# A recurrence in units of two steps: paired values on two row groups of the array, one VectorE product for two

## The reference

```
o_t[j] = sum_i r_t[i] * (s[i,j] + exp(u[i] + k_t[i]) * v_t[j])
s[i,j] = exp(w_t[i]) * s[i,j] + k_t[i] * v_t[j]
```

## Time and profile before

| | us |
|---|---|
| Median of 3 runs | 2596.15 (2594.57 to 2597.19) |
| Profiled execution | 2599.8, span 2598.0 |
| A woven stage (seven) | 208.2 |
| Recurrence alone (last) | 153 |
| Busy: PE, DVE, ACT, POOL | 2043.4, 1638.1, 845.2, 607.8 |

### The profile page before, as it was taken

The page is one execution under the profiler, slowest core; times in us unless marked ns, Lnnn a source line. Parts: engine busy times, 40 slices in busy tenths (PEclk is TensorE's granted clock), DMA queues, the critical chain, the costliest instruction groups (busy, mean ns, idle before and its releaser), DMA issues. The chain is left out here.

```text
span 2598.0 us, 29698 instructions
## 1 busy us (share of the span) xinstructions
PE 2043.4 (79%) x10381; PEld 1319.8 (51%) x10444; DVE 1638.1 (63%) x2846; ACT 845.2 (33%) x1530; POOL 607.8 (23%) x357
## 2 busy tenths in 40 slices
PE   0865985896796797697599588655279999999998
PEld 0543554454354454454455445422157777777775
DVE  3234696696597588679569669658355555455554
ACT  0342352353333333344235235320133222322222
POOL 0000243143044033233224314315111220112010
PEclk9686897897897888789789789775589999999999
DMA  4000000000000000000000000000210000000000
GB/s 120 1 1 8 1 1 17 1 1 9 9 1 9 9 1 1 17 1 1 17 1 1 17 1 1 1 8 0 65 53 22 17 17 17 0 17 16 16 1 17
DMA packets 32290, 33.24 MB, mean 13 GB/s; under 512 B 4496, under 2 KB 31184, under 8 KB 31952
## 3 DMA queue, kind: packets, MB, share of 16 engines
q1 hardware_dynamic: 32144, 31.38, 3.9%
HBM read 22.99 MB, written 8.39 MB: 12 GB/s over the span
## 5 line engine op out<-in xcount | busy, mean ns | idle before, releaser
L557 DVE TENSOR_TENSOR_SCAN s_buf<-r_work,kvb 128x512 f32<-128x512 f32 x256 | 363.9, 1422 | 0.0
L655 POOL TENSOR_TENSOR p_buf<-s_buf,r_work 128x512 f32<-128x512 f32 x128 | 151.9, 1187 | 511.5 <-DVE s_buf L557 511.5
L1525 PE MATMUL mbank<-m_xh,w_hi 128*128 128x512 f32 x544 | 229.5, 422 | 0.1
L1333 DVE TENSOR_TENSOR hl<-hf,hh 128x512 fp32r<-128x512 f32 x136 | 94.0, 691 | 201.1 <-ACT hh L1440 200.4
L655 POOL TENSOR_TENSOR r_work<-s_buf,r_work 128x512 f32<-128x512 f32 x128 | 165.1, 1290 | 229.1 <-DVE s_buf L557 229.1
L710 ACT ACTIVATE probs<-bank_s,nmx 128x256 f32<-128x256 f32 (+1 forms) x512 | 186.9, 451 | 94.2 <-DVE nmx L420 90.6
L1525 PE MATMUL mbank<-m_xl,w_hi 128*128 128x512 f32 x544 | 216.5, 398 | 0.0
L1525 PE MATMUL mbank<-m_xh,w_lo 128*128 128x512 f32 x544 | 216.2, 397 | 0.0
L728 ACT ACTIVATE pt<-bank_s 128x1024 f32<-128x1024 f32 (+1 forms) x128 | 117.5, 918 | 248.5 <-PE bank_s L972 248.5
L546 DVE TENSOR_TENSOR kvb<-r_work,bank 128x512 f32<-128x512 f32 x256 | 174.7, 682 | 23.7 <-PE bank L1070 13.1
L1436 ACT ACTIVATE sg<-mbank 128x512 f32<-128x512 f32 x136 | 81.5, 599 | 327.6 <-PE mbank L1525 327.6
(11 more groups left out here) (247 smaller groups left out, 4155.0 us busy)
## 6 DMA issues: line engine op xcount, KB each, us to landing
w_raw<-in_w SPq DMA_DIRECT2D x17, 256.0 KB, 2.7
x_new<-in_x SPq DMA_DIRECT2D x8, 512.0 KB, 3.3
x_after_rwkv<-x_b SPq DMA_DIRECT2D x8, 512.0 KB, 3.7
m_x_tok<-x_after_rwkv SPq DMA_DIRECT2D x8, 512.0 KB, 3.8
out<-m_x_tok SPq DMA_DIRECT2D x8, 512.0 KB, 2.9
w_raw<-in_w2e SPq DMA_DIRECT2D x17, 128.0 KB, 2.7
work<-in_w SPq DMA_DIRECT2D x2, 1024.0 KB
wrk<-in_wrk SPq DMA_DIRECT2D x1, 1024.0 KB
```

The costliest lines, as they stand in the source:

```text
L557: V.tensor_tensor_scan(s_buf[:, n % 2, 1:S + 1], dec[:, n // HD, :], kvb[:, n % 2, :], 0.0, ALU.mult, ALU.add).then_inc(sem["state"], 1)
L655: G.tensor_tensor(p_slot(n), s_buf[:, n % 2, 0:S], rf[:, n // HD, :], ALU.mult).then_inc(sem["rs"], 1)
L1333: V.tensor_tensor(hl[:, e % 3, :], hf[:, e % 3, :], hh[:, e % 3, :].bitcast(F32), ALU.subtract).then_inc(sem["h_lo"], 1)
L1525: ins = T.matmul(o, w[:, e, cols:cols + P], m, start=first and c == 0, stop=last and c == 2)
```

## The change

The recurrence goes in 16 units m of two steps. v stays fp32 (`v_f`); v_hi and v_lo are gone, as are a ScalarE copy and a VectorE subtraction for each group. `sel_v` shrinks to four matrices, made by three adds in place of one cast. A unit takes two fp32 matmuls over 32 rows each, in neighbouring row groups, into the two banks R0 and R1, which now form one tensor (`spread_banks`); one VectorE product takes both banks at once (`kvb` becomes twice as large). There are two scans and two GpSimd products a unit, as before. On VectorE a unit goes scan, scan, and then the product of the next one. There is one set of spread banks: unit m+1 is spread after the product of m, and the first spreading waits for the bonus product. The four strings are new.

```diff
-    tensor="araarrrrarrrararrararrarararrararrararrarrarraraarrararraararrarararararaaarrraarrararraaaarrarrraaraaraaaaaraa",
-    vector="arararrrrarrraaraarrrrrararararrararrararrarraararrararraararraraarrararaaararrararrrrarararaaarraaraaraaaaaraa",
-    scalar="aarrrrrarrraarrarraararaarraraarrrrraaaaarrrraraararraaaarrraarrrarraraararrrrraaaararrrarrrrraaararaaraaaraaaa",
-    gpsimd="arararrarrraaaarrrarrraarrrrrraararrraaararaarrrrararaaaaaraarraararrrrrarrarraaaaraaarrrrraarrrarrraaraaaaaraa",
+    tensor="raaarrrrrarrararrarararaaararaarararaararararaararaaraararaararrarraraaarrararaaararaararaaaaaa",
+    vector="ararrrarrrarararrrraaaaraararaarararaararararaararaaararaaaararraarrrararrraaarraaaraaraaaaraaa",
+    scalar="ararrrarrrrararrraaaaraaraaaaararaaararrrraraaararaarrrarararaaaaaaaarraarrarrrararraaaraaaaara",
+    gpsimd="ararrarrraaaarararrrrrarrararaaaaraarrraarararraraaraaaaaarrraaaaaaaaaarrrrraaaaararrarraraaara",
...
-        bank = [score_banks[i // 2][:, i % 2, :] for i in range(4)] + [ctx.enter_context(nc.psum_tensor(f"bank{i}", [P, 512], F32)) for i in range(4, 8)]
+        bank = [score_banks[i // 2][:, i % 2, :] for i in range(4)]
+        bank += [ctx.enter_context(nc.psum_tensor("bank4", [P, 512], F32))]
+        spread_banks = ctx.enter_context(nc.psum_tensor("bank_r", [P, 2, 512], F32))
+        bank += [spread_banks[:, 0, :], spread_banks[:, 1, :], ctx.enter_context(nc.psum_tensor("bank7", [P, 512], F32))]
...
-        sel_v = sb("sel_v", [P, HD, P], F32R)
+        sel_v = sb("sel_v", [P, 4, P])
...
-            V.tensor_copy(sel_v[:].rearrange("p a m -> p (a m)"), raw[:, 4096:6144])
+            sel_part = lambda c: raw[:, 4096 + 512 * c:4608 + 512 * c].rearrange("p (a m) -> p a m", a=4)
+            own.link(V.tensor_tensor(sel_v[:], sel_part(0), sel_part(1), ALU.add))
+            own.link(V.tensor_tensor(sel_v[:], sel_v[:], sel_part(2), ALU.add))
+            V.tensor_tensor(sel_v[:], sel_v[:], sel_part(3), ALU.add)
...
-                for g in range(2):
-                    ve.wait_ge(sem["v_f"], at(b, "v_f", g + 1))
-                    ins = V.tensor_tensor(v_lo[:, g, :], vf[:, g, :], v_hi[:, g, :].bitcast(F32), ALU.subtract)
-                ins.then_inc(sem["v_lo"], 1)
+                kf, ek, dec, rf = (r_work[:, i:i + 2, :] for i in (2, 4, 6, 8))
...
-                def kv(n):
-                    ve.wait_ge(sem["v_bc"], at(b, "v_bc", n + 1))
-                    if n >= 2:
-                        ve.wait_ge(sem["state"], at(b, "state", n - 1))
-                    V.tensor_tensor(kvb[:, n % 2, :], kf[:, n // HD, :], RB[n % 2][:], ALU.mult).then_inc(sem["kv"], 1)
+                pair = lambda ap, m: bc(ap[:, m // (N_SCAN // 2), :].unsqueeze(1), P, 2, S)
+
+                def kv(m):
+                    ve.wait_ge(sem["v_bc"], at(b, "v_bc", m + 1))
+                    if m >= 2:
+                        ve.wait_ge(sem["state"], at(b, "state", 2 * m - 2))
+                    V.tensor_tensor(kvb[:, m % 2], pair(kf, m), spread_banks[:], ALU.mult).then_inc(sem["kv"], 1)
 
                 kv(0)
                 yield "rspread"
-                for n in range(N_SCAN + 2):
-                    if n + 1 < N_SCAN:
-                        kv(n + 1)
-                    if n < N_SCAN:
-                        ve.wait_ge(sem["kv"], at(b, "kv", n + 1))
-                        if n >= 2:
-                            ve.wait_ge(sem["rs"], at(b, "rs", n - 1))
-                        V.tensor_tensor_scan(s_buf[:, n % 2, 1:S + 1], dec[:, n // HD, :], kvb[:, n % 2, :], 0.0, ALU.mult, ALU.add
-                                             ).then_inc(sem["state"], 1)
-                    if n > 1 and n % HD == 1:
-                        g = n // HD - 1
+                for m in range(N_SCAN + 2):
+                    if m < N_SCAN:
+                        ve.wait_ge(sem["kv"], at(b, "kv", m + 1))
+                        for x in range(2):
+                            if m >= 2:
+                                ve.wait_ge(sem["rs"], at(b, "rs", 2 * m - 3 + x))
+                            V.tensor_tensor_scan(s_buf[:, m % 2, x, 1:S + 1], dec[:, m // (N_SCAN // 2), :], kvb[:, m % 2, x], 0.0, ALU.mult, ALU.add
+                                                 ).then_inc(sem["state"], 1)
+                    if m + 1 < N_SCAN:
+                        kv(m + 1)
+                    if m in (10, 17):
+                        g = m // 17
...
-                    n = int(name[4:]) if name.startswith("scan") else -1
-                    if 0 <= n < N_SCAN:
-                        gp.wait_ge(sem["state"], at(b, "state", n + 1))
-                        if n >= 8:
-                            gp.wait_ge(sem["summed"], at(b, "summed", n // 4 - 1))
-                        G.tensor_tensor(p_slot(n), s_buf[:, n % 2, 0:S], rf[:, n // HD, :], ALU.mult).then_inc(sem["rs"], 1)
+                    m = int(name[4:]) if name.startswith("scan") else -1
+                    if 0 <= m < N_SCAN:
+                        if m >= 4:
+                            gp.wait_ge(sem["summed"], at(b, "summed", m // 2 - 1))
+                        for x in range(2):
+                            gp.wait_ge(sem["state"], at(b, "state", 2 * m + 1 + x))
+                            G.tensor_tensor(p_slot(m)[:, x, :], s_buf[:, m % 2, x, 0:S], rf[:, m // (N_SCAN // 2), :], ALU.mult
+                                            ).then_inc(sem["rs"], 1)
...
-                    A(v_hi[:, g, :], RB[(2 + g) % 3][:], ACT.Copy)
-                    A(vf[:, g, :], RB[(2 + g) % 3][:], ACT.Copy).then_inc(sem["v_f"], 1)
+                    A(v_f[:, g, :], RB[(2 + g) % 3][:], ACT.Copy).then_inc(sem["v_f"], 1)
...
-                def spread_v(n):
-                    g, j = n // HD, row_of(n)
-                    if n >= 2:
-                        pe.wait_ge(sem["kv"], at(b, "kv", n - 1))
-                    T.matmul(RB[n % 2][:], sel_v[:, j, :], v_hi[:, g, :], start=True, stop=False)
-                    T.matmul(RB[n % 2][:], sel_v[:, j, :], v_lo[:, g, :], start=False, stop=True).then_inc(sem["v_bc"], 1)
-
-                pe.wait_ge(sem["v_lo"], at(b, "v_lo", 1))
+                def spread_v(m):
+                    g, a = m // (N_SCAN // 2), m % (N_SCAN // 2) // 2
+                    if m:
+                        pe.wait_ge(sem["kv"], at(b, "kv", m))
+                    for x in range(2):
+                        c = 2 * (m % 2) + x
+                        ins = T.matmul(spread_banks[:, x, :], sel_v[32 * c:32 * c + 32, a, :], v_f[32 * c:32 * c + 32, g, :], start=True, stop=True)
+                    ins.then_inc(sem["v_bc"], 1)
+
+                pe.wait_ge(sem["bonus"], at(b, "bonus", 1))
                 spread_v(0)
-                pe.wait_ge(sem["bonus"], at(b, "bonus", 1))
-                spread_v(1)
                 yield "rspread"
-                for n in range(N_SCAN + 2):
-                    if n >= 5 and n % 4 == 1:
-                        quad = n // 4 - 1
+                for m in range(N_SCAN + 2):
+                    if m >= 3 and m % 2 == 1:
+                        quad = m // 2 - 1
                         g, a = divmod(quad, 4)
                         pe.wait_ge(sem["rs"], at(b, "rs", 4 * quad + 4))
                         if a == 0 and g:
                             pe.wait_ge(sem["o_sb"], at(b, "o_sb", g))
                         for c in range(4):
-                            ins = T.matmul(R2[32 * c:32 * c + 32, :], sel_sum[:, a, :], p_slot(4 * quad + c),
+                            ins = T.matmul(R2[32 * c:32 * c + 32, :], sel_sum[:, a, :], p_slot(2 * quad + c // 2)[:, c % 2, :],
                                            start=a == 0, stop=a == 3)
                         ins.then_inc(sem["summed"], 1)
-                    if n + 2 < N_SCAN:
-                        spread_v(n + 2)
-                    yield f"scan{n}"
+                    if m + 1 < N_SCAN:
+                        spread_v(m + 1)
```

More of the change, by code:

```diff
@@ L27 @@
 QUADS = 4
+N_SCAN = HD
 N_LOC = QUADS * NT
@@ L203, in mid_token_layers @@
         r_small = sb("r_small", [P, 5, 64])
-        v_hi = sb("v_hi", [P, NK, S], F32R)
-        v_lo = sb("v_lo", [P, NK, S], F32R)
-        kvb = sb("kvb", [P, 2, S])
-        s_buf = sb("s_buf", [P, 2, S + 2])
+        v_f = sb("v_f", [P, NK, S])
+        kvb = sb("kvb", [P, 2, 2, S])
+        s_buf = sb("s_buf", [P, 2, 2, S + 2])
         p_buf = sb("p_buf", [P, 4, S])
-        ones = s_buf[:, 0, 0:P]
+        ones = s_buf[:, 0, 0, 0:P]
         xn, y_tok = work[:, 10:12, :], work[:, 0:2, :]
@@ L563, in rwkv_head @@
                         V.tensor_tensor(o_f[:, g, :], o_f[:, g, :], R2[:], ALU.add).then_inc(sem["o_sb"], 1)
-                    if n == N_SCAN + 1:
+                    if m == N_SCAN + 1:
                         own.end()
-                    yield f"scan{n}"
+                    yield f"scan{m}"
             def rwkv_tail(b):
@@ L765, in rwkv_head @@
             def rwkv_head(b):
```

(2 more changed lines are left out.)

22 lines of the change are left out of this document (9 added, 13 removed).

## The result

| | before | after |
|---|---|---|
| Median of the runs | 2596.67 (4 runs) | 2668.88 (2634.19 to 2678.79, 4 runs) |
| Profiled execution | 2599.8, span 2598.0 | 2678.79, span 2676.6 |
| Ratio | | 1.0233, 95% interval 1.0136 to 1.033 |
| Busy: PE, DVE, ACT, POOL | 2043.4, 1638.1, 845.2, 607.8 | 2100.6, 1567.8, 835.2, 680.6 |

The changed kernel is 2.3% slower, by a first series whose interval is wide; 2586 was predicted. The profiled execution is the longest of the four, 1.7% above the shortest, and the ratio leaves it out.

What follows compares the result with a forecast made beforehand. TensorE was taken to bound the stretch before the first row maximum, VectorE the local attention, TensorE close behind. Seven stages -7.0, last stage -4.1, setup +1.0: together -10.1, giving a median of 2586 us, range 2555 to 2625.

Steps and rivals of the forecast that it cites:

- the stretch of the local attention: First to 16th row maximum of a stage: 68.7 us against 67.6, +1.1, with four more scans done.
- rival 3: Local attention: TensorE, with less to do, granted the half clock for two of 15 blocks a stage; 2635 us, chance 0.12.
- TensorE's spreading: Two fp32 matmuls side by side take 0.95 us a pair of steps against 1.6; TensorE gives back 10 us a stage.
- rival 4: Spreading on TensorE: the two matmuls run one after the other, 1.7 us, +8 a stage; 2649 us, chance 0.06.
- The VectorE product: Recurrence on VectorE: 16 products of 1024 replace 32 of 512, 19.2 to 18.2 us, saving 1.0 a batch.
- The order scan, scan, product: Last stage: a pair takes 4.33 us against 4.69, first spreading waits +1.3; together -4.1 us.
- Stretch 914.3 to 938.8: Bonus product to first row maximum, TensorE-bound: first row maximum 2.4 us earlier a stage, bounds 0 and -4.0.
- The end: Behind the 16th row maximum: gate's reduction ends 13.9 us after it, before 13.8, so zero; 0.3 shows in the FFN.
- Setup: VectorE's setup: one cast of 1.22 us becomes three adds of about 0.69 each, with a wait; +1.0 us.
- Hidden: v_hi's copies and v_lo's subtraction, 1.2 us a batch each on ScalarE and VectorE, lie beside TensorE's projections, which don't stop.
- Rival 1: Better kept: both engines shed work, the 1.4 us idles and the +1.1 go, -4.5 a stage; 2561 us, chance 0.22.
- Rival 2: Single set of spread banks delays the product, 5.2 a stage, 2622 us, chance 0.18; test: wait above 5 us a stage.

Runs made afterwards that it cites:

- e3: Changed kernel with its TensorE part undone: high and low part in fp32r over 128 rows, v_hi and v_lo back; 2582.22 us, ratio 0.9933.
- g3: Kernel before with only the rows changed: each fp32r spreading matmul over 32 rows in place of 128; 2678.89 us, ratio 1.031.
- f2: e3 with each of a unit's four matmuls over 32 rows, the two steps side by side; 2620.35 us, ratio 1.0095.
- g1: e3 timed again, same program; 2585.41 us, ratio 0.9952.
- f4: e3 with two VectorE products of 512 in place of one of 1024; 2599.72 us, ratio 1.0004.
- e1: Kernel before with the spreading matmul of the low part of v left out; 2636.7 us, ratio 1.0123.
- h1: Changed kernel itself timed again, nothing altered; 2667.26 us, ratio 1.0252.

## Why the prediction was wrong, step by step

The step that failed is *the stretch of the local attention*: 68.7 us were predicted from issue intervals, all of them taken at a granted clock of 1.00, and 80.7 came at 0.81. The VectorE arithmetic of that step was right: at full clock the blocks follow in 4.5 us, and e3 took 67.4 at 1.00 (69.6 in the mean of its seven stages). One count in it is off without effect: three more scans fall in the stretch than before (26 for 23), not four. The clock of the earlier trace rows was carried over to a kernel whose matmuls were no longer the same. This was *rival 3*, which I gave 0.12 and priced at two blocks a stage, 2635. The half clock lasted 30 us of the local stretch, some five blocks, and 2669 came. It also rested on the wrong reason: I thought of TensorE having less to do, while in the trace it is busy 28.74 of 30 us at 0.50. What changed is the height of the matmuls (g3 alone, +82 us; f2 against e3, +38). A sign stood in the rows of the kernel before and was read past: in the first line of the earlier trace rows TensorE is busy for 24.50 of 24.50 us at a clock of 0.66. The prediction counted this 0.66 for waits between groups of matmuls, but there is no wait in that stretch.

*TensorE's spreading* failed in the other direction. I took 0.80 us for a high/low pair, from 986.01 to the next row at 986.81, and doubled it. That row isn't the next matmul. The kernel issues two mask matmuls there (L918, `for x in range(2)`), and the row says x1: the record of the first is missing. In the whole trace L918 has 256 weight loads and 193 matmul records; in g1 and g3 all 256 are there. Where both are recorded, a lone pair of the kernel before takes 0.57 us:

```profile
L918 PEld LDWEIGHTS bank_s<-wmask,ident_b x256: 95/98/151, 107.5 to 1627.8; 128*128 128x128 bf16 x128
L918 PE MATMUL bank_s<-wmask,ident_b x193: 272/379/634, 107.5 to 1628.0; 128*128 128x512 bf16 x129, 128*128 128x256 bf16 x64
...
964.02 0.50 PE L1069 MATMUL bank<-v_hi,sel_v 128*128 128x512 f32 x1
...
964.59 0.61 PE L918 MATMUL bank_s<-wmask,ident_b 128*128 128x512 bf16 x2
```

What two pairs take stood in the next rows of the kernel before, which follow the last of the earlier trace rows, at 989.78:

```profile
990.12 0.39 PE L1070 MATMUL bank<-v_lo,sel_v 128*128 128x512 f32 x1
990.35 0.39 PE L1069 MATMUL bank<-v_hi,sel_v 128*128 128x512 f32 x1
990.58 0.40 PE L1070 MATMUL bank<-v_lo,sel_v 128*128 128x512 f32 x1
990.82 0.39 PE L918 MATMUL bank_s<-wmask,ident_b 128*128 128x256 bf16 x2
```

989.78 to 990.82 = 1.04 us, not 1.6. The new form was sized well (0.95 predicted, 1.06 measured, side by side, so *rival 4* is out), but it relieves TensorE of next to nothing: the 10 us a stage never existed (two lone pairs, 1.14, would make it 1.3). By the same missing record the block of attention, 2.97 us in the prediction, takes 3.2, so that "it just fits" had no ground. The change gave up the height of its matmuls for no time worth having.

- *The VectorE product*: 1.14 us a unit predicted, records of 1.199, issued 1.11 ahead of the next instruction (959.16 to 960.27). Its worth was put at 1.0 a batch, 8 in all. Undoing it (f4) costs 14 to 20, most of it where no product stands and where f4's clock is a little lower; its worth by itself isn't separated.
- *The order scan, scan, product*: right. 4.31 us a pair for 4.33; from the bonus product to the end of the last scan 71.6 us against 75.95, -4.4 for -4.1.
- *Stretch 914.3 to 938.8*: from bonus product to first row maximum 20.0 us against 20.8 in the stage read, -0.8 for the -2.4, at 0.66 and 0.67. But that stage is one of four; in the three others of the kernel before the part takes 17.7 us, TensorE as busy:

```profile
709.80:727.51 17.71, 17.70 (x98) 13.11 (x97) 15.69 (x19) 2.73 (x5) 6.13 (x6) 0.81 0.00 0
```

  Over the seven stages it is 138.6 us against 136.4: +2.2, where -17 was forecast. The term fails, outside its bounds (0 and -4.0 a stage), and the clock is in it too: the changed kernel has 0.66 in six of the seven. In e3 the sum is 128.6.
- *The end*: 16th row maximum to the end of the gate's reduction 13.6 against 13.8; what follows to the next power operation +0.5 for +0.3. *Setup*: the three adds start at 38.6, 39.3 and 40.0 us, +0.7 at the first row maximum for +1.0. *Hidden*: nothing of it shows, and it wasn't measured apart.
- *Rival 1* stayed out of reach even where the clock held: e3's 2582 lies above 2561. Its price doesn't come out of its terms either: with the idle of 2.8 gone a stage gains 3.8, not 4.5, which makes 2566. *Rival 2*: its own test came out positive (7.5 us) and was misleading; e3 has the same banks, 1.4 us of that wait, and is fast.
- The count: forecast -10.1; with TensorE's part undone, e3 and g1 show -17.4 and -11.9. That this is near the forecast is partly luck. In e3's profile the seven local stretches are 8.8 us longer than before (+7.7 forecast), the parts in front of them 7.8 shorter (-17 forecast), the six parts from the 16th row maximum to the next bonus product 8.0 shorter (some +2 forecast), and the end of the recurrence, from the last row maximum to the last scan, 5.9 shorter (-4.1 forecast for the last stage). With the TensorE part, +78.1 in the local stretches.

What stays open: which property of the 32-row matmuls the clock answers to. The runs show that height matters at equal columns, count and kind, and that less full-height work costs clock too (e1). They don't show how much of f2's loss is the order of its four matmuls, nor a rule from which one could compute it. Why the stages of e3 alternate between 1.00 and 0.94 is open as well, and a second set of spread banks wasn't tried.

## What to carry to other kernels

A sum of instruction times is made at one granted clock; before it is trusted for an edit on TensorE, ask whether the edit keeps what holds the clock, and give the other level a full price (here about 7 us for each 0.10 of clock in a local stretch, by h1). Before you read a gap between two rows as occupation, count the records against the matmuls that the source issues there; a missing one had turned 0.57 us into 0.80. Read more than one stage: those of the kernel before differ by 3 us in one part. And when an edit has independent parts, time each alone: the part on VectorE was worth -0.5 to -0.7%, the part on TensorE +3.2 to +3.4%.
